# Values' products of all units in two parts, the feed-forward product in two parts beside them, shared banks by a fixed table

## The chip, the cores and the metric

The kernel runs on one core of a Trainium2 chip. Its five engines each run their own instruction stream, in order: TensorE (PE; its weight loads are PEld), VectorE (DVE), ScalarE (ACT), GpSimd (POOL) and SyncE (SP), which here issues DMAs. They wait for each other through semaphores. The metric is the device time of one execution in microseconds, median of several.

## The reference

One layer on x of shape (16, 512, 256), float32. After a layer norm without parameters, attention and a feed-forward product run side by side, and both are added to x:

```python
xn = _layernorm(x, axis=-1)
qkv = xn @ w_qkv.T + b_qkv                      # 16 heads of 16
att = einsum('bhqd,bhkd->bhqk', q, k) / sqrt(16) + hope_bias
att = softmax(where(causal, att, -inf))
attn = einsum('bhqk,bhkd->bhqd', att, v) @ w_proj.T + b_proj
ffn = fp8(bf16(xn) / s_in) @ fp8(kernel / s_k) * (s_in * s_k)   # rounded to bf16, + bias
out = x + attn + ffn
```

The position bias depends on the distance of query and key and on the head.

## The kernel before

The body of the loop handles one batch row b (of 16): the first is written out, a loop runs over bodies 1 to 13, and the last two are written out. A body has G = 4 units g (0 to 3) of four heads each, and a unit has SLOTS = 12 slots k. In each slot (g, k) TensorE computes two blocks: transposed scores of this unit (`scores_T`, L648, and L651 for the position features of units 0 and 1; banks scoreT_a, b, c in turn), which ScalarE turns into probabilities by an exponential (L1013), and plain scores for two units ahead (`scores`, L625; banks score_a, b, c in turn), of which VectorE takes the row maxima (L1101). Slots 0 to 3 have 512 columns, slots 4 to 7 384, slots 8 to 11 384 in two pieces. Slot k of either kind needs the exponential, or the maximum, of slot k - 3, which frees its bank. GpSimd masks the diagonal of the probabilities (L1324).

Between slots TensorE does jobs in two shared banks, misc_a and misc_b, whose slots stand in the tables `*_AT` at the head of the file:

- PV, the product of values and probabilities of the unit before (`pv`, L674; fp32, four heads beside each other in 32 columns each). Its first part (key tile 0, 512 columns) needs only the first mask; the rest (tiles 1 to 3) the other two. Each fp32 matmul leaves two records, so the first part has 8 and the rest 24. In unit 0 and unit 1 the first part stands behind slot 0 and the rest behind slot 3; in units 2 and 3 both stand behind slot 3.
- MT, the transposition of the next unit's row maxima (`job_MT`, L610 and L611). It waits for ScalarE's copy of them (`max_hi`, L908, ahead of the exponential of slot 2). In units 2 and 3 it is issued between the first part of PV and the rest, in unit 1 ahead of the rest, in unit 0 behind it. ScalarE copies it out (L914), SyncE sends it by DMA, and scores_T of the next unit wait for it.
- QK and V, projections of the next row (`job_QK`, `job_V`, L560), units 0, 1 and unit 2; FF, the feed-forward product (`job_FF`, L603), both halves behind slot 0 of unit 2; PJ, the output projection of the row before (`job_PJ`, L560), halves behind slots 0 and 6 of unit 3; T, transpositions of xn (`job_T`, L568), behind slot 9 of unit 3.

Each job waits until what the job before it left in its bank has been read (`misc`, `done`): for FF ScalarE's eviction (L1036), for PV ScalarE's `out_T` (L986, ahead of the exponential of slot 4), for PJ VectorE's addition to x (`result`, L1114, behind the maximum of slot 1 or 6), for V ScalarE's L887, for QK VectorE's L1089, for MT ScalarE's L914. The order of all jobs over a body is `ORDER`, and before, the two banks simply alternate along it. In units 2 and 3 that gives:

```
FF0 a, FF1 b | PV1 a, MT2 b | V0 a | V1 b || PJ0 a | PV2 b, MT3 a | PJ1 b | T0 a, T1 b
```

Of the kernel before, what the change touches and what calls it, by code (L numbers as in the profile page):

```python
# [27 lines left out]
B, T, C = 16, 512, 256  # L28
H, HD = 16, 16
TT = T // P  # L30
# [18 lines left out]

PV_AT = [(1, 0), (2, 3), (3, 3), (0, 0)]

PV_REST_AT = {0: (1, 3), 3: (0, 3)}
MT_AT, FIRST_MT_AT = [(0, 3), (1, 3), (2, 3), (3, 3)], (0, 2)
QK_AT = [(0, 6), (0, 9), (1, 6), (1, 9)]
V_AT = [(2, 6), (2, 9)]
FF_AT = [(2, 0), (2, 0)]
PJ_AT = [(3, 0), (3, 6)]
T_AT = (3, 9)  # L60

# [5 lines left out]
QK_HI_AT, QK_LO_AT = [(0, 6), (0, 9), (1, 6), (1, 9)], [(0, 7), (0, 10), (1, 7), (1, 10)]  # L67
V_OUT_AT = [(2, 6), (2, 9)]
AH_AT = [(2, 2), (2, 3)]
FF_OUT_AT = [(2, 0), (2, 1)]  # L70
RESULT_AT = [(3, 1), (3, 6)]
NORM_AT = [(3, 1), (3, 3), (3, 4), (3, 6)]
XH_AT = [(3, 9), (3, 10)]
# [7 lines left out]

FIRST_CHUNKS = [0, 1, 4, 5, 8, 9, 2, 3, 6, 7, 10, 11]

KINDS = ("PV", "MT", "QK", "V", "FF", "PJ", "T")
ORDER = [(KINDS[kind], i) for _, kind, i in sorted((at, kind, i) for kind, ats in enumerate(
    (PV_AT, MT_AT, QK_AT, V_AT, FF_AT, PJ_AT, [T_AT, T_AT])) for i, at in enumerate(ats))]
assert len(ORDER) % 2 == 0
MISC_BANK = {job: n % 2 for n, job in enumerate(ORDER)}
MASKED = -1.0e30
LEAST = -3.0e38  # L90

# [18 lines left out]
def due(jobs, g, k, lag=0):  # L110

    return [i for i, (jg, jk) in enumerate(jobs) if SLOTS * jg + jk == SLOTS * g + k - lag]
# [13 lines left out]
def build(nc, x, w_qkv, b_qkv, w_proj, b_proj, pos, ffn_w, s_in, s_k, ffn_b, feat_q, feat_k, out):  # L126
    with ExitStack() as ctx:
# [199 lines left out]
        def misc_of(kind, i):  # L327

            return MBS[MISC_BANK[kind, i]]

# [206 lines left out]
        def _(pe):  # L537
# [33 lines left out]
            def job_QK(b, m):  # L571

                col = P * [0, 2, 1, 3][m]
                if m == 0:
                    pe.wait_ge(xl_ready, 2 * (b + 1))
                bank = misc("QK", m, b - 1)
                split3(bank[:, :], (lambda ct: WH[:, ct, col:col + P], lambda ct: WL[:, ct, col:col + P]),
                       (lambda ct: XH[:, ct, :], lambda ct: XL[:, ct, :]), T).then_inc(qk_ready, 1)
# [84 lines left out]
            def pv(b, g, tiles, then):  # L663
                if 0 in tiles:
                    if g == 0:
                        pe.wait_ge(va_ready, b + 1)
                    misc("PV", g, b if g < 3 else b + 1)
                elif then and g < 3:
                    job_MT(*then)
                bank = misc_of("PV", g)  # L670
                for j in tiles:
                    pe.wait_ge(mask_done, 12 * b + 3 * g + min(j, 2) + 1)
                    for i in range(HU):
                        last = mm(bank[32 * i:32 * i + 32, P * j:T],  # L674
                                  VA[:, j, HU * g + i, :, :].rearrange("p d a -> p (d a)"),
                                  probs(g, j)[:, i, :], start=(j == 0), stop=(j == TT - 1))
                    if j == 0 and then:
                        job_MT(*then)
                if TT - 1 in tiles:
                    last.then_inc(pv_done, 1)  # L680
                if 0 not in tiles and then and g == 3:
                    job_MT(*then)
# [106 lines left out]
            def body(b, first, last, more):  # L789
                if not first and not last:  # L790
                    for n in range(2):
                        job = [x for x in ORDER if MISC_BANK[x] == n][-1]
                        bank_read[n] = done(*job, b - 1)
                for g in range(G):
                    nb, ng = (b, g + 2) if g < 2 else (b + 1, g - 2)
                    ahead = not (last and g >= 2)
                    for k in range(SLOTS):
                        pb, pg = (b, g - 1) if g else (b - 1, 3)
                        if ahead:
                            in_turn(scores_T(b, g, k, first), scores(nb, ng, k))  # L800
                        else:
                            in_turn(scores_T(b, g, k, first))
                        if not (first and g == 0):
                            then = None if last and g == 3 else (b, g + 1) if g < 3 else (b + 1, 0)
                            if (g, k) == PV_AT[pg]:
                                pv(pb, pg, range(1) if pg in PV_REST_AT else range(TT), None if pg in PV_REST_AT else then)
                            if pg in PV_REST_AT and (g, k) == PV_REST_AT[pg]:
                                pv(pb, pg, range(1, TT), then)
                        if first and (g, k) == FIRST_MT_AT:
                            job_MT(b, 1)  # L810
                        if last and (g, k) == LAST_DENOMINATORS_AT:
                            pe.wait_ge(max_done, ROW * B)
                            last_denominators(2)
                        if last and (g, k) == LAST_INVERSES_AT:
                            last_inverses(2)
                        if not last:
                            for i in due(QK_AT, g, k):
                                job_QK(b + 1, i)
                            for i in due(V_AT, g, k):
                                job_V(b + 1, i)  # L820
                        for i in due(FF_AT, g, k):
                            job_FF(b, i)
                        if not first:
                            for i in due(PJ_AT, g, k):
                                job_PJ(b - 1, i)
                        if (g, k) == T_AT and more:
                            for i in range(CT):
                                job_T(b + 2, i)
# [42 lines left out]
        def _(act):  # L871
# [122 lines left out]
            def body(b, first, last, more):  # L994
                for g in range(G):
                    for k in range(SLOTS):
                        pb, pg = (b, g - 1) if g else (b - 1, 3)
                        if (g, k) == FIRST_MAX_AT if first and g == 0 else k == MAX_AT:
                            if not (last and g == 3):
                                max_hi(*((b, g + 1) if g < 3 else (b + 1, 0)))  # L1000
                        if k == OUT_AT and not (first and g == 0):
                            if g == 0:
                                out_T(pb, pg, False)
                            if not (last and g == 3):
                                max_T(*((b, g + 1) if g < 3 else (b + 1, 0)))
                            if g > 0:
                                out_T(pb, pg, first and pg == 0)
                        act.wait_ge(st_ready, ROW * b + SLOTS * g + k + 1)
                        if first and (g, k) == (0, 4):
                            for i in range(2):  # L1010
                                act.wait_ge(feat_loaded[i], 64)
                        w = WJ[k // 4] if k < 8 else WJ[2] + WJ[3]
                        A(probs_slot(g, k), STB[(SLOTS * g + k) % 3][:, 0:w], ACT.Exp).then_inc(exp_done, 1)  # L1013
                        if first and (g, k) == FIRST_MT_OUT_AT:
                            max_T(b, 1)
                        if not last:
                            for i in due(QK_HI_AT, g, k):
                                QK_evac(b + 1, i)
                            for i in due(V_OUT_AT, g, k):
                                V_evac(b + 1, i)  # L1020
                        if more:
                            for t in due(NORM_AT, g, k):
                                normalise(b + 2, t)
                            for i in due(XH_AT, g, k):
                                XH_evac(b + 2, i)
                                if i == 0:
                                    act.wait_ge(xy_ready, b + 1)
                                XB_evac(b + 2, i)
                        if not first:
                            for ct in due(AH_AT, g, k):  # L1030
                                attn_hi(b - 1, ct)
                        for i in due(FF_OUT_AT, g, k):
                            act.wait_ge(ff_ready, 2 * b + i + 1)
                            if i == 0 and not last:
                                act.wait_ge(qz_done, b + 2)
                            A(Y1[:, 2 * i:2 * i + 2, :], misc_of("FF", i)[:, :].rearrange("p (t c) -> p t c", c=C),  # L1036
                              ACT.Identity, scale=SC[:, 3:4]).then_inc(y1_ready, 1)

            body(0, True, False, True)
            with act.Fori(1, B - 2) as b:  # L1040
# [449 lines left out]
```

## Time and profile before

| | us |
|---|---|
| median of 3 runs (766.87 to 767.3) | 767.23 |
| profiled execution | 769.2 |
| its span | 767.2 |
| TensorE busy | 738.7 |
| VectorE busy | 634.6 |
| ScalarE busy | 586.1 |
| GpSimd busy | 532.4 |

An engine is busy while an instruction of it runs; ends of matmuls are modelled, so start times say more of TensorE than its busy time. A row of the timeline is: start, duration in us, engine, line, operation, output <- inputs, shapes, count; in square brackets the engine's idle time ahead of it and what ended it.

### The profile page before, as it was taken

The page shows a single profiled execution, that of the slowest core. Times are in us where ns is not written, and L with a number is a line of the kernel's source. Part 1 is how long each engine was busy: PE and PEld are TensorE (multiplying, and loading weights), DVE is VectorE, ACT ScalarE, POOL GpSimd, SP SyncE. Part 2 cuts the span into 40 slices and gives each one's busy share as a digit, 9 for nine tenths or more (in the row PEclk, how much of TensorE's full clock was granted, in tenths as well). Part 3 has the DMA queues.
Part 4 walks back from the last instruction along what each step waited for, and adds up shares of the span by engine and source line. Part 5 has one row for each costly group of instructions (what it writes and reads, how often), then busy time and mean ns, then how long its engine had stood idle before and what let it go on. Part 6 is the DMA issues. An engine that isn't in the chain of part 4 may idle for free.

```text
span 767.2 us, 23128 instructions
## 1 busy us (share of the span) xinstructions
PE 738.7 (96%) x6285; PEld 475.1 (62%) x6285; DVE 634.6 (83%) x2401; ACT 586.1 (76%) x1263; POOL 532.4 (69%) x525
## 2 busy tenths in 40 slices
PE   7989999999999999999999999999999999999987
PEld 4656556666765666566566656666665666666555
DVE  4898798889989888988988898898988889888613
ACT  4557888787888878788887878878787888877662
POOL 7445767786777778776777868677776867767571
PEclk9999999999999999999999999999999999999889
DMA  5442353435335433533544253244425334443201
GB/s 181 150 152 103 128 176 142 139 118 178 117 138 174 153 127 118 184 128 121 174 153 141 112 187 136 108 170 152 158 95 193 133 120 153 160 148 108 88 32 62
DMA packets 55313, 105.65 MB, mean 138 GB/s; under 512 B 10421, under 2 KB 30389, under 8 KB 55285
## 3 DMA queue, kind: packets, MB, share of 16 engines
q1 hardware_dynamic: 53968, 104.52, 38.3%
q10 hardware_dynamic: 1316, 0.80, 0.4%
q8 instruction: 13, 0.21, 0.1%
q14 instruction: 16, 0.12, 0.1%
HBM read 18.42 MB, written 8.90 MB: 36 GB/s over the span
## 4 chain that ended last, share of the span: by engine, by line
PE 68%; ACT 11%; DVE 8%; issue 6%; DMA 2%; SPq 2%; DVEq 1%; ACTq 1%; POOLq 0%; POOL 0%
PE misc_a L560 13%; PE misc_a L674 10%; PE misc_b L560 9%; PE scoreT_b L648 9%; PE scoreT_a L648 5%; PE score_c L625 4%; PE misc_b L674 3%; ACT probs L1013 3%; PE score_a L625 2%; PE scoreT_b L651 2%; ACT qk_parts L901 2%; ACT attn_hi L992 2%; DVE row_max L1101 2%; SPq L351 1%; ACT out_T L986 1%
## 5 line engine op out<-in xcount | busy, mean ns | idle before, releaser
L1324 POOL TENSOR_SCALAR_AFFINE_SELECT probs<-probs 128x512 f32<-128x512 f32 x256 | 161.1, 640 | 185.7 <-ACT probs L1013 184.0
L1101 DVE CUSTOM_DVE_ANT_0 score_b<-score_b,causal_mask_q 128x384 f32<-128x384 f32 (+3 forms) x321 | 162.7, 523 | 80.6 <-PE score_b L625 80.3
L1101 DVE CUSTOM_DVE_ANT_0 score_a<-score_a,causal_mask_q 128x512 f32<-128x512 f32 x319 | 174.6, 563 | 2.9 <-PE score_a L625 2.8
L1101 DVE CUSTOM_DVE_ANT_0 score_c<-score_c,causal_mask_q 128x256 f32<-128x256 f32 (+3 forms) x384 | 172.0, 475 | 0.1
L1013 ACT ACTIVATE probs<-scoreT_b 128x384 f32<-128x384 f32 (+1 forms) x256 | 131.8, 515 | 44.7 <-PE scoreT_b L651 21.2
L1013 ACT ACTIVATE probs<-scoreT_a 128x512 f32<-128x512 f32 (+1 forms) x256 | 142.6, 557 | 9.3 <-PE scoreT_a L651 8.0
L1101 DVE DVE_READ_ACCUMULATOR2_ANT row_max<- 128x1 f32 x1024 | 142.8, 139 | 0.0
L1013 ACT ACTIVATE probs<-scoreT_c 128x384 f32<-128x384 f32 (+1 forms) x256 | 133.3, 521 | 1.5 <-PE scoreT_a L648 0.9
L674 PE MATMUL misc_a<-probs,v_ones 128*32 128x128 f32 (+3 forms) x1536 | 124.1, 441 | 3.5 <-DVE xnT_lo L1083 1.3
L648 PE MATMUL scoreT_b<-stacks 64*128 64x384 f32 (+3 forms) x320 | 120.6, 396 | 1.6 <-ACT probs L1013 1.5
L625 PE MATMUL score_b<-stacks 64*128 64x384 f32 (+3 forms) x321 | 116.0, 394 | 0.0
L648 PE MATMUL scoreT_a<-stacks 64*128 64x512 f32 (+3 forms) x320 | 106.6, 353 | 5.5 <-issue 2.1
L625 PE MATMUL score_a<-stacks 64*128 64x512 f32 x319 | 107.9, 370 | 0.3
L648 PEld LDWEIGHTS scoreT_b<-stacks 64*128 64x128 f32 x320 | 56.6, 184 | 77.4 <-ACT probs L1013 45.1
L648 PE MATMUL scoreT_c<-stacks 64*128 64x256 f32 (+3 forms) x384 | 102.4, 299 | 0.3 <-ACT probs L1013 0.3
L625 PE MATMUL score_c<-stacks 64*128 64x256 f32 (+3 forms) x384 | 94.5, 299 | 0.9 <-DVE row_max L1101 0.8
L674 PEld LDWEIGHTS misc_a<-probs,v_ones 128*32 128x32 f32 x1536 | 40.2, 109 | 54.0 <-issue 32.8
L648 PEld LDWEIGHTS scoreT_c<-stacks 64*128 64x128 f32 x384 | 68.6, 186 | 1.2 <-ACT probs L1013 0.9
L625 PEld LDWEIGHTS score_c<-stacks 64*128 64x128 f32 x384 | 65.5, 186 | 5.7 <-DVE row_max L1101 4.4
L625 PEld LDWEIGHTS score_a<-stacks 64*128 64x128 f32 x319 | 54.5, 186 | 15.6 <-DVE row_max L1101 11.1
L648 PEld LDWEIGHTS scoreT_a<-stacks 64*128 64x128 f32 x320 | 57.2, 186 | 11.2 <-issue 5.0
L625 PEld LDWEIGHTS score_b<-stacks 64*128 64x128 f32 x321 | 54.2, 184 | 1.4 <-DVE row_max L1101 1.1
(238 smaller groups left out, 1937.4 us busy)
## 6 DMA issues: line engine op xcount, KB each, us to landing
stacks<-qk_parts SPq DMA_DIRECT2D x128, 512.0 KB, 3.7
x_ring<-in_L_attn_x SPq DMA_DIRECT2D x16, 512.0 KB, 3.6
attn<-out_T SPq DMA_DIRECT2D x63, 128.0 KB, 2.6
xn<-recips SPq DMA_DIRECT2D x31, 256.0 KB
out<-x_ring SPq DMA_DIRECT2D x15, 512.0 KB, 3.0
stacks<-neg_max_T SPq DMA_DIRECT2D x128, 4.0 KB
low_features<-neg_max_T SPq DMA_DIRECT2D x126, 4.0 KB
low_features<-probs SPq DMA_DIRECT2D x8, 128.0 KB, 4.3
```

Source lines behind the costliest of these rows:

```text
L351: eng.dma_start(max_rows(g, h), MTS[2 * TT * h:2 * TT * h + 2 * TT, g % 2, :].bitcast(F32)) \
L560: last = mm(o, l(ct), r(ct), start=(ct == 0 and i == 0), stop=(ct == CT - 1 and i == 2))
L625: last = mm(SB_[n % 3][:, o:o + w], STK[rows, u, 0, P * qt:P * qt + P], STK[rows, u, 1, 0:w], start=True, stop=True)
L648: last = mm(bank, STK[rows, u, 1, P * j:P * j + P], STK[rows, u, 0, P * j:T], start=True, stop=(g >= 2))
L651: last = mm(bank, EXT[rows, u, 1, P * j:P * j + P], EXT[rows, u, 0, P * j:T], start=False, stop=True)
L674: last = mm(bank[32 * i:32 * i + 32, P * j:T], VA[:, j, HU * g + i, :, :].rearrange("p d a -> p (d a)"), probs(g, j)[:, i, :], start=(j == ...
L901: A(qk_part(m, 0), misc_of("QK", m)[:, :].unsqueeze(1).broadcast_to([P, 2, T]), ACT.Identity, bias=BQ[:, bias:bias + 1]).then_inc(qh_ready, 1)
L986: A(OT[:, :], misc_of("PV", g)[:, :], ACT.Copy).then_inc(ot_ready, 1)
L992: A(AH[:, ct, :], attn_row(b)[:, ct, :], ACT.Copy).then_inc(ah_ready, 1)
L1013: A(probs_slot(g, k), STB[(SLOTS * g + k) % 3][:, 0:w], ACT.Exp).then_inc(exp_done, 1)
L1101: last = V.tensor_tensor_reduce(bank, bank, CMQ[:, T - w:T], 1.0, LEAST, ALU.add, ALU.max, MX[:, g % 2, 8 * h + 4 + qt:8 * h + 5 + qt])
L1324: last = GP.affine_select(out=d, in_=d, compare_op=ALU.is_ge, fill=0.0, base=0, pattern=[[0, HU], [1, P]], channel_multiplier=-1)
```

## The change

All four products of values are in two parts: the first part behind slot 0, the rest behind slot 3. MT is issued with the rest (ahead of it in units 1 to 3, behind it in unit 0). The second half of the feed-forward product and its eviction move from slots (2, 0) and (2, 1) to (2, 6); it stands ahead of the values' projection there, and its eviction ahead of ScalarE's other evictions. The banks come from a table in place of the alternation; PV is always in misc_a, MT, FF and PJ in misc_b. Units 2 and 3 become:

```
PV1 a, FF0 b | MT2 b | FF1 b, V0 a | V1 b || PV2 a, PJ0 b | MT3 b | PJ1 b | T0 a, T1 b
```

```diff
-PV_AT = [(1, 0), (2, 3), (3, 3), (0, 0)]
-PV_REST_AT = {0: (1, 3), 3: (0, 3)}
+PV_AT = [(1, 0), (2, 0), (3, 0), (0, 0)]
+PV_REST_AT = [(1, 3), (2, 3), (3, 3), (0, 3)]
-FF_AT = [(2, 0), (2, 0)]
+FF_AT = [(2, 0), (2, 6)]
-FF_OUT_AT = [(2, 0), (2, 1)]
+FF_OUT_AT = [(2, 0), (2, 6)]
-KINDS = ("PV", "MT", "QK", "V", "FF", "PJ", "T")
+KINDS = ("PV", "MT", "QK", "FF", "V", "PJ", "T")
-MISC_BANK = {job: n % 2 for n, job in enumerate(ORDER)}
+MISC_BANK = {(kind, i): bank for kind, banks in (("PV", (0, 0, 0, 0)), ("MT", (1, 1, 1, 1)), ("QK", (0, 1, 0, 1)), ("FF", (1, 1)),
+                                                 ("V", (0, 1)), ("PJ", (1, 1)), ("T", (0, 1))) for i, bank in enumerate(banks)}
...
                             if (g, k) == PV_AT[pg]:
-                                pv(pb, pg, range(1) if pg in PV_REST_AT else range(TT), None if pg in PV_REST_AT else then)
-                            if pg in PV_REST_AT and (g, k) == PV_REST_AT[pg]:
+                                pv(pb, pg, range(1), None)
+                            if (g, k) == PV_REST_AT[pg]:
                                 pv(pb, pg, range(1, TT), then)
...
+                        for i in due(FF_AT, g, k):
+                            job_FF(b, i)
+                        if not last:
                             for i in due(V_AT, g, k):
                                 job_V(b + 1, i)
-                        for i in due(FF_AT, g, k):
-                            job_FF(b, i)
...
                         A(probs_slot(g, k), STB[(SLOTS * g + k) % 3][:, 0:w], ACT.Exp).then_inc(exp_done, 1)
...
+                        for i in due(FF_OUT_AT, g, k):
+                            act.wait_ge(ff_ready, 2 * b + i + 1)
+                            ...
                         if not last:
                             for i in due(QK_HI_AT, g, k):
                                 QK_evac(b + 1, i)
...
                                 attn_hi(b - 1, ct)
-                        for i in due(FF_OUT_AT, g, k):
-                            ...
```

## Rows read from the trace of the kernel before

**Rows 1.** The profile's page: busy time, granted clock in 40 slices, chain by engine.
```profile
PE 738.7 (96%) x6285; PEld 475.1 (62%) x6285; DVE 634.6 (83%) x2401; ACT 586.1 (76%) x1263; POOL 532.4 (69%) x525
...
PEclk9999999999999999999999999999999999999889
...
PE 68%; ACT 11%; DVE 8%; issue 6%; DMA 2%; SPq 2%; DVEq 1%; ACTq 1%; POOLq 0%; POOL 0%
```
**Rows 2.** Waits of TensorE: us in total, times, longest.
```profile
PE misc_a L610 <- DVE x_ring L1114: 2.3, 14, 0.2
```
**Rows 3.** Timeline of TensorE: the transpositions T that close two neighbouring bodies.
```profile
262.23 0.66 PE L568 MATMUL misc_a<-ident_f,xn 128*128 128x128 f32 x4
...
306.67 0.66 PE L568 MATMUL misc_a<-ident_f,xn 128*128 128x128 f32 x4
```
**Rows 4.** Timeline of TensorE, a body's unit 3, slots 0 to 3.
```profile
298.07 0.38 PE L560 MATMUL misc_a<-w_projT_hi,attn_hi 128*128 128x256 f32 x1
298.29 0.28 PE L560 MATMUL misc_a<-w_projT_lo,attn_hi 128*128 128x256 f32 x1
...
299.68 0.50 PE L625 MATMUL score_b<-stacks 64*128 64x512 f32 x1
...
300.58 1.06 PE L674 MATMUL misc_b<-probs,v_ones 128*32 128x512 f32 x8
301.81 0.27 PE L610 MATMUL misc_a<-ident_f,row_max 128*32 128x128 f32 x1 [0.16 <-DVE x_ring L1114]
...
302.06 1.50 PE L674 MATMUL misc_b<-probs,v_ones 128*32 128x384 f32 x24
```
**Rows 5.** Timeline of VectorE and ScalarE in the same unit.
```profile
300.36 0.70 DVE L1101 CUSTOM_DVE_ANT_0 score_b<-score_b,causal_mask_q 128x512 f32<-128x512 f32 x1 [0.55 <-PE score_b L625]
300.97 0.69 DVE L1114 TENSOR_TENSOR x_ring<-misc_a,x_ring 128x512 f32 x1
301.20 0.22 ACT L908 ACTIVATE row_max_hi<-row_max 128x32 fp32r<-128x32 f32 x1
...
304.11 0.57 DVE L1101 CUSTOM_DVE_ANT_0 score_b<-score_b,causal_mask_q 128x384 f32<-128x384 f32 x1 [1.14 <-PE score_b L625]
```
**Rows 6.** Timeline of TensorE, unit 1: first part of PV behind slot 0.
```profile
276.01 1.07 PE L674 MATMUL misc_a<-probs,v_ones 128*32 128x512 f32 x8
277.00 0.50 PE L648 MATMUL scoreT_b<-stacks 64*128 64x512 f32 x1
```
**Rows 7.** Timeline of unit 2, slots 0 to 6: TensorE, ScalarE and VectorE.
```profile
287.06 0.61 PE L603 MATMUL misc_a<-ffn_w_q,xq 128*128 128x256 bf16 x4
...
287.86 0.61 PE L603 MATMUL misc_b<-ffn_w_q,xq 128*128 128x256 bf16 x4 [0.20 <-DVE qk_parts L1089]
...
288.40 0.49 PE L648 MATMUL scoreT_b<-stacks 64*128 64x512 f32 x1
...
288.93 0.60 ACT L1013 ACTIVATE probs<-scoreT_b 128x512 f32<-128x512 f32 x1 [0.16 <-PE scoreT_b L648]
...
289.08 0.70 DVE L1101 CUSTOM_DVE_ANT_0 score_b<-score_b,causal_mask_q 128x512 f32<-128x512 f32 x1
...
289.43 0.68 ACT L1036 ACTIVATE xnT_bf<-misc_b,ffn_scales 128x512 bf16<-128x512 f32 x1
...
290.00 0.23 ACT L908 ACTIVATE row_max_hi<-row_max 128x32 fp32r<-128x32 f32 x1
...
290.57 0.28 PE L610 MATMUL misc_b<-ident_f,row_max 128*32 128x128 f32 x1
...
292.73 0.34 PE L648 MATMUL scoreT_a<-stacks 64*128 64x384 f32 x1
...
293.20 0.39 PE L560 MATMUL misc_a<-w_qkvT_hi,xnT_hi 128*128 128x256 f32 x1
```
**Rows 8.** Timeline of the first body's unit 3.
```profile
78.07 0.26 ACT L908 ACTIVATE row_max_hi<-row_max 128x32 fp32r<-128x32 f32 x1
...
79.39 0.28 PE L610 MATMUL misc_a<-ident_f,row_max 128*32 128x128 f32 x1
```
**Rows 9.** Timeline of TensorE, the last body's unit 3, slot 0.
```profile
738.55 0.79 PE L648 MATMUL scoreT_a<-stacks 64*128 64x512 f32 x1 [0.93 <-DMA stacks<-neg_max_T]
```

More of the change, by code:

```diff
@@ L82 @@
 FIRST_CHUNKS = [0, 1, 4, 5, 8, 9, 2, 3, 6, 7, 10, 11]
-KINDS = ("PV", "MT", "QK", "V", "FF", "PJ", "T")
+KINDS = ("PV", "MT", "QK", "FF", "V", "PJ", "T")
 ORDER = [(KINDS[kind], i) for _, kind, i in sorted((at, kind, i) for kind, ats in enumerate(
-    (PV_AT, MT_AT, QK_AT, V_AT, FF_AT, PJ_AT, [T_AT, T_AT])) for i, at in enumerate(ats))]
-assert len(ORDER) % 2 == 0
-MISC_BANK = {job: n % 2 for n, job in enumerate(ORDER)}
+    (PV_AT, MT_AT, QK_AT, FF_AT, V_AT, PJ_AT, [T_AT, T_AT])) for i, at in enumerate(ats))]
+MISC_BANK = {(kind, i): bank for kind, banks in (("PV", (0, 0, 0, 0)), ("MT", (1, 1, 1, 1)), ("QK", (0, 1, 0, 1)), ("FF", (1, 1)),
+                                                 ("V", (0, 1)), ("PJ", (1, 1)), ("T", (0, 1))) for i, bank in enumerate(banks)}
 MASKED = -1.0e30
@@ L1015, in body @@
                             max_T(b, 1)
+                        for i in due(FF_OUT_AT, g, k):
+                            act.wait_ge(ff_ready, 2 * b + i + 1)
+                            if i == 0 and not last:
+                                act.wait_ge(qz_done, b + 2)
+                            A(Y1[:, 2 * i:2 * i + 2, :], misc_of("FF", i)[:, :].rearrange("p (t c) -> p t c", c=C),
+                              ACT.Identity, scale=SC[:, 3:4]).then_inc(y1_ready, 1)
                         if not last:
@@ L1031, in body @@
                                 attn_hi(b - 1, ct)
-                        for i in due(FF_OUT_AT, g, k):
[L1033 to L1037, printed above, removed]
             body(0, True, False, True)
```

## Prediction

> **What bounds the kernel now.** The profile's page first. TensorE is busy for 96% of the span and holds 68% of the chain that ended last, at full clock everywhere but near the end [rows 1]. The list of TensorE's own waits has one entry that matters here: fourteen times the transposition of the row maxima (L610, in misc_a) waits 0.2 us for VectorE's addition at L1114 [rows 2]. The timeline gives the body of the loop: from the transpositions that close one body to those of the next is 306.67 - 262.23 = 44.44 us [rows 3]. A body has four units of twelve slots. In most of them TensorE starts a job right behind the last, and ScalarE and VectorE follow it; so whatever TensorE issues more, or waits for longer, lengthens the body, unless it stood idle there anyway. I therefore follow TensorE's start times through units 2 and 3, where all edits lie.
>
> **Unit 3 (the third unit's product of values).** Before, slot 0 is followed by the first half of the projection (298.07); slot 1's scores start at 299.68; slots 1 to 3 take 0.90; at 300.58 comes the first part of the product (8 records), at 301.81 the transposed maxima (MT), at 302.06 the rest [rows 4]. What releases MT is a chain that starts at slot 1's scores: VectorE takes their maximum at 300.36, then adds the projection to x at 300.97 (0.69), and 0.15 behind its end MT starts, since MT takes the bank that the projection used. VectorE had been idle 0.55 before that maximum, waiting for the scores [rows 5]. ScalarE's leg is nearly as long: the copy of the maxima starts at 301.20, takes 0.22, and with the same 0.15 allows MT at 301.57 [rows 5]. So from slot 1's scores to MT are 301.81 - 299.68 = 2.13 us, and the first part of the product was hidden in them. TensorE waited only 0.16.
>
> The change puts that first part behind slot 0, ahead of the projection, and MT ahead of the rest. Both are in misc_b's chain again (projection's half, then MT), so the wait for L1114 stays. What the first part costs at slot 0 is seen in unit 1, where it stands there already: 277.00 - 276.01 = 0.99 [rows 6]. Slot 1 therefore starts 1.0 later. The 2.13 us from there to MT belong to VectorE and ScalarE and do not shrink; only their cover is gone: TensorE has 0.90 of scores and then waits about 1.23. MT, and all behind it, comes 1.0 later. Nothing behind it gives that back: VectorE is idle for 1.14 before slot 4's maximum, waiting for TensorE [rows 5]. Sum of unit 3: +1.0. Bounds: if VectorE's leg ran faster ScalarE's would bind, 0.24 earlier, so +0.75; if the 1.23 from the first part's start to MT [rows 4] were all lost, +1.23. I take 1.0, since unit 1 has the same instructions in the same place.
>
> **Unit 2 (the second unit's product, feed-forward product).** Before: both halves of the feed-forward product behind slot 0, 287.06 and 287.86, the second after a wait of 0.20 for VectorE; slot 1 at 288.40; MT at 290.57 behind the first part; slot 6's scores at 292.73; values' projection at 293.20 [rows 7]. A half costs 288.40 - 287.86 = 0.54. After: first part 287.06 to 288.05, one half to 288.6 (its bank, misc_b, is free by then, so the wait of 0.20 goes), slot 1 at 288.6, 0.2 later than before. ScalarE evicts the half from about 288.75, and by the starts of rows 7 (an eviction 290.00 - 289.43 = 0.57, an exponential 289.43 - 288.93 = 0.50) copies the maxima at 288.75 + 0.57 + 0.50 = 289.82, which allows MT 0.37 later (0.22 and 0.15), at 290.19. That is 0.38 earlier than before, though TensorE has idled some 0.65 for it. Not all of it is kept: slot 6's scores need slot 3's maximum, VectorE's maxima run back to back there (289.08 right behind the one before), and slot 1's is now 0.2 late. I estimate slot 6 at 292.5, so 0.2 are left of the 0.38. Behind it stands the second half of the feed-forward product, 0.54 less the change of shape (0.1, below) that the values' projection next to it no longer pays, and less the 0.13 that TensorE stood there before the values' projection (293.20 - 292.73 = 0.47 for a block of 0.34): +0.3. I take +0.1 for the unit. Bounds: -0.38 if the second half is wholly hidden, +0.54 if nothing hides it.
>
> **The rest.** Units 0 and 1 have had the product in two parts already, and their jobs keep their banks. In unit 3 the second half of the projection moves behind MT in misc_b, where it waited for the product's eviction before: nothing to a few hundredths. ScalarE's second eviction of the feed-forward product moves to slot 6, into the time it waits for the values; the wait for a free bank that it adds there is for a value written long before. GpSimd's bias addition (L1330) stands behind a mask of slot 7, after slot 6's eviction. SyncE's queue keeps its order; the maxima it sends come 0.4 earlier in unit 2 and 1.0 later in unit 3, with the unit that wants them as far behind as before.
>
> **Ends.** The projection exists from the second body on, and the last body has no MT in unit 3: fourteen bodies pay unit 3, the number of rows 2. In the first body MT (79.39) comes 1.3 after the copy of the maxima at 78.07 [rows 8], so that unit had slack and the first part moves free of charge: +0.1 for unit 2 alone. In the last body unit 3 starts behind a wait for the sent maxima (0.93, [rows 9]), which ScalarE's later copy passes on: +0.3, with half-clock stretches near the end that can fall differently, 3 us either way.
>
> Sum: 14 x (1.0 + 0.1) + 0.1 + 0.3 = 15.8 us. The profiled execution took 769.2 (span 767.2), the timed ones 767.23; the sum is small beside both, so 769.2 becomes 785.0 and the median 783.0.
>
> **A rule against the change.** The first matmul of the projection is followed after 0.22 (298.07 to 298.29), while all twelve take 1.61 [rows 4], 0.126 for each of the others: a change of tile shape costs about 0.1. The Trainium skill, TensorEngine Tiling, Key Properties, says that changing the tiling mode drains TensorE; the trace agrees. By that rule each of units 2 and 3 pays one more change, 14 x 2 x 0.1 = 2.8 us. In my sum unit 3's is inside the 0.99 and unit 2's inside a wait; paid on top in unit 2 it would make 784.4.
>
> **Rivals.** (a) The first part moves into a hole. In the first body it does [rows 8]. Were TensorE also idle around slot 0 in the full bodies, unit 3 would lose nothing and unit 2 keep its 0.38: 14 x -0.38 = -5.3, 761.9. It decides if the longer wait for MT in unit 3 is under 0.4. Against it: VectorE idle 0.55 before slot 1's maximum waits on TensorE, not the reverse [rows 5]. 4%. (b) The loss is given back in slots 4 to 11, no change: VectorE and ScalarE would have to be the late ones there, and the 1.14 says the opposite. 3%. (c) The fixed table makes new waits: feed-forward, values, projection and MT now follow each other in misc_b, each behind an eviction, and nothing of unit 2 is hidden: 14 x (1.0 + 0.54) + 0.4 = 22, 789.2. Between each pair lie at least three slots or a first part. 10%. (d) The clock. A wait of 0.93 in the last body is followed by a block of scores of 0.79 where the same block takes 0.49 [rows 7, 9], that is at half clock; a slice of 19.2 us with the digit 8 [rows 1] holds 4 to 8 us of it. A wait of 1.23 in each body might do the same: up to 3 us of doubled work each, 14 x 3 + 16 = 58, 825. For it speaks only that row; around unit 3 TensorE is otherwise full. 5%. (e) Unit 3's chain shortens and unit 2 gains: 14 x (0.75 - 0.38) = 5, 772.6. 5%.
>
> **Numbers.** My forecast, 779 to 787: 73%. Range 775 to 790: it takes in most of (c), and leaves out (a), (b), (d) and (e), about 17 in 100. What this kernel's measurement can tell from no change is 0.2%, 1.5 us. Faster 4% (a), same 3% (b), slower 93%.
>
> **What would show it.** In unit 3 the first part directly behind slot 0; the gap between slot 3's scores and MT about 1.2 us, released by L1114; 2.1 us from slot 1's scores to MT. In unit 2 MT about 3.1 us behind slot 0's job, released by ScalarE's copy, where it was 3.51. A body of 45.5 us. I am wrong if MT in unit 3 starts under 1.8 us behind slot 1's scores, if the body is under 44.9, or if the granted clock leaves 1.0 in the loop.

## The result, and the profile after

| | before | after |
|---|---|---|
| median, us | 767.26 (766.87 to 768.08, 4 runs) | 792.01 (787.52 to 797.75, 4 runs) |
| profiled execution, us | 769.2 | 793.55 |
| its span, us | 767.2 | 791.8 |
| body of the loop, us | 44.44 | 45.4 in most, 47.1 in others |

The ratio is 1.0325, interval [1.0255, 1.0396]: 24.8 us slower. I had said 783.0 and a range of 775 to 790, so the direction was right, and the size was not. And the changed kernel spreads over 10 us in four runs, where the one before spread over 1.2 (and over 6.7 in the 25 runs beside e5 to e8).

The page after, against [rows 1]: busy times, granted clock, chain.

```profile
PE 742.1 (94%) x6285; PEld 480.4 (61%) x6285; DVE 644.5 (81%) x2401; ACT 585.2 (74%) x1263; POOL 527.6 (67%) x525
...
PEclk9999999999999999999999999999999999999889
...
PE 80%; issue 6%; ACT 5%; DVE 5%; DMA 2%; SPq 2%; DVEq 0%; POOL 0%; ACTq 0%; POOLq 0%
```

The number of instructions is the same. The page shows little more: TensorE's share fell by two points, VectorE is busy 10 us longer although it does nothing new. That is the first hint at something other than waits. TensorE's waits after (engine, tile, line, what it waited for; us in total, times, longest), against [rows 2]:

```profile
PE misc_b L611 <- DVE x_ring L1116: 16.3, 14, 1.2
PE misc_b L611 <- ACT row_max_hi L910: 9.9, 19, 0.7
PE score_b L626 <- DVE row_max L1103: 3.4, 6, 0.6
```

(Lines from L611 on are one or two further down than before.) The first row is [rows 2] grown from 2.3 to 16.3 us, 1.2 for each of the same fourteen bodies: the wait that the prediction put there. The second was 0.5 before: it is mostly MT of unit 2, which now waits for ScalarE's copy (0.54 in the body shown below); the sum had allowed 0.65 for that. The third is new and was in no rival of mine: six times slot 7's scores of unit 2 wait for a maximum. The bodies, from the transpositions that close one to the next:

```profile
219.38 0.55 PE L569 MATMUL misc_a<-ident_f,xn 128*128 128x128 f32 x3
...
266.48 0.33 PE L569 MATMUL misc_a<-ident_f,xn 128*128 128x128 f32 x1
...
311.86 0.66 PE L569 MATMUL misc_a<-ident_f,xn 128*128 128x128 f32 x4
```

The second body takes 45.38 us, 0.94 more than before; the first 47.10, another 1.72. Four bodies of the profiled execution take 47.0 to 47.2 and a fifth 48.56; a sixth of the kind stands behind the last of these transpositions, so there are six in fourteen.

**Unit 3 after**, TensorE, VectorE and ScalarE, against [rows 4, 5]:

```profile
302.32 1.06 PE L675 MATMUL misc_a<-probs,v_ones 128*32 128x512 f32 x8
303.32 0.38 PE L561 MATMUL misc_b<-w_projT_hi,attn_hi 128*128 128x256 f32 x1
...
304.93 0.49 PE L626 MATMUL score_b<-stacks 64*128 64x512 f32 x1
...
305.60 0.70 DVE L1103 CUSTOM_DVE_ANT_0 score_b<-score_b,causal_mask_q 128x512 f32<-128x512 f32 x1 [1.53 <-PE score_b L626]
306.21 0.69 DVE L1116 TENSOR_TENSOR x_ring<-misc_b,x_ring 128x512 f32 x1
306.44 0.22 ACT L910 ACTIVATE row_max_hi<-row_max 128x32 fp32r<-128x32 f32 x1
307.05 0.27 PE L611 MATMUL misc_b<-ident_f,row_max 128*32 128x128 f32 x1 [1.17 <-DVE x_ring L1116]
...
309.36 0.57 DVE L1103 CUSTOM_DVE_ANT_0 score_b<-score_b,causal_mask_q 128x384 f32<-128x384 f32 x1 [1.14 <-PE score_b L626]
```

The first part costs 1.00 ahead of the projection; from slot 1's scores to MT are 2.12 (before 2.13), with nothing in them but scores; VectorE's idle time at slot 1 grew from 0.55 to 1.53, and at slot 4 it is 1.14 as before, so nothing came back.

**Unit 2 after**, a body of the short kind, against [rows 7]; the last two rows are VectorE's second quantisation step and GpSimd's subtraction:

```profile
291.30 1.07 PE L675 MATMUL misc_a<-probs,v_ones 128*32 128x512 f32 x8
292.30 0.61 PE L604 MATMUL misc_b<-ffn_w_q,xq 128*128 128x256 bf16 x4
292.84 0.50 PE L649 MATMUL scoreT_b<-stacks 64*128 64x512 f32 x1
...
293.03 0.69 ACT L1022 ACTIVATE xnT_bf<-misc_b,ffn_scales 128x512 bf16<-128x512 f32 x1 [0.58 <-PE misc_b L604]
...
294.09 0.23 ACT L910 ACTIVATE row_max_hi<-row_max 128x32 fp32r<-128x32 f32 x1
...
294.45 0.28 PE L611 MATMUL misc_b<-ident_f,row_max 128*32 128x128 f32 x1 [0.54 <-ACT row_max_hi L910]
...
297.12 0.61 PE L604 MATMUL misc_b<-ffn_w_q,xq 128*128 128x256 bf16 x4
...
296.56 0.69 DVE L1132 SCALAR_TENSOR_TENSOR quant_work<-xn,quant_work 128x512 f32<-128x512 f32 x1
...
296.56 2.93 POOL L1365 TENSOR_TENSOR attn_lo<-attn,attn_hi 128x1024 fp32r<-128x1024 f32 x1
```

MT is 3.15 behind slot 0's job, before 3.51: 0.36 earlier, where I had 0.38. Slot 6's scores come 5.46 behind it (before 5.67, forecast 5.44) and the values' projection 6.19 (before 6.14). The whole body is 0.94 longer, the sum's 1.1 less 0.16.

**The collision.** The same two instructions in a body of the kernel before, with GpSimd's mask ahead of them, and in one of the long kind after, with the maximum and the scores that follow:

```profile
291.85 0.64 POOL L1324 TENSOR_SCALAR_AFFINE_SELECT probs<-probs 128x512 f32<-128x512 f32 x1 [0.92 <-ACT probs L1013]
...
292.12 0.92 DVE L1130 SCALAR_TENSOR_TENSOR quant_work<-xn,quant_work 128x512 f32<-128x512 f32 x1
...
292.47 2.82 POOL L1363 TENSOR_TENSOR attn_lo<-attn,attn_hi 128x1024 fp32r<-128x1024 f32 x1
```

```profile
249.54 2.38 POOL L1365 TENSOR_TENSOR attn_lo<-attn,attn_hi 128x1024 fp32r<-128x1024 f32 x1
...
249.57 2.90 DVE L1132 SCALAR_TENSOR_TENSOR quant_work<-xn,quant_work 128x512 f32<-128x512 f32 x1
252.39 0.55 DVE L1103 CUSTOM_DVE_ANT_0 score_b<-score_b,causal_mask_q 128x384 f32<-128x384 f32 x1
...
253.06 0.44 PE L626 MATMUL score_b<-stacks 64*128 64x384 f32 x1 [0.53 <-DVE row_max L1103]
```

Both instructions read two operands from SBUF, the memory on the chip that the program keeps its tiles in. The one that starts later is held up by the other. Before, VectorE's step starts 0.35 ahead of the subtraction, and the subtraction is drawn out from 2.38 to 2.82, which nobody waits for; it ends 2.25 behind the step's end. That the step takes 0.92 there and not 0.69 is a smaller collision of the same kind, with the mask: the mask is running when the step starts, and the step ends 0.55 behind the mask's end (291.85 + 0.64 = 292.49, against 293.04). In e10 one step takes 0.94 with the mask alone beside it, since the subtraction is held back there. After, the subtraction starts 0.03 ahead and takes 2.38, and VectorE's step takes 2.90, 2.2 more than its 0.69, and ends 0.55 behind the subtraction's end. The maxima of slots 4 to 6 stand behind it, and TensorE's slots 7 and 8 behind those.

The edits brought the two together. Counted from the job behind slot 0 of unit 2, VectorE's step started at 292.12 - 287.06 = 5.06 and GpSimd's at 5.41 before; after (the short body above) both at 296.56 - 291.30 = 5.26. VectorE comes 0.20 later, since slot 1's scores do, and GpSimd 0.15 earlier, since ScalarE is no longer held by the second eviction of the feed-forward product: a margin of 0.35 became 0.00. The subtraction follows the mask directly, so what decides is whether the step starts before the mask is over: 0.37 before its end in the kernel before, at its very end now. Which one wins then changes from body to body and run to run: six bodies of fourteen here. The spread between runs follows it: four runs spread over 5.0 us in e1, which still has the collision, and over some 2 in e5 and e9, which have not.

### The profile page after: what moved, and what is told of

It reads as the page before. It is cut to its first block, busy times and chain, and to the rows that moved or that the text cites. A ratio compares the mean times of both kernels' runs of the same rounds, so it can differ in the third digit from the quotient of the medians.

```text
span 791.8 us, 23128 instructions
## 1 busy us (share of the span) xinstructions
PE 742.1 (94%) x6285; PEld 480.4 (61%) x6285; DVE 644.5 (81%) x2401; ACT 585.2 (74%) x1263; POOL 527.6 (67%) x525
## 4 chain that ended last, share of the span: by engine, by line
PE 80%; issue 6%; ACT 5%; DVE 5%; DMA 2%; SPq 2%; DVEq 0%; POOL 0%; ACTq 0%; POOLq 0%
PE misc_a L675 19%; PE misc_b L561 15%; PE scoreT_b L649 10%; PE misc_a L561 8%; PE scoreT_a L649 6%; PE score_c L626 4%; PE score_a L626 3%; PE scoreT_b L652 2%; PE misc_b L611 2%; PE misc_b L604 2%; PE scoreT_a L652 1%; PE scoreT_c L652 1%; ACT probs L1015 1%; DVE xnT_lo L1085 1%; PE scoreT_c L649 1%
## 5 line engine op out<-in xcount | busy, mean ns | idle before, releaser
L675 PE MATMUL misc_a<-probs,v_ones 128*32 128x512 f32 (+3 forms) x2048 | 166.3, 442 | 3.5 <-POOL probs L1326 1.1
L1103 DVE DVE_READ_ACCUMULATOR2_ANT row_max<- 128x1 f32 x1024 | 145.5, 142 | 0.0
L626 PE MATMUL score_a<-stacks 64*128 64x512 f32 x319 | 109.7, 375 | 0.4
L649 PE MATMUL scoreT_c<-stacks 64*128 64x256 f32 (+3 forms) x384 | 104.0, 302 | 0.3 <-ACT probs L1015 0.3
L675 PEld LDWEIGHTS misc_a<-probs,v_ones 128*32 128x32 f32 x2048 | 53.6, 109 | 70.2 <-issue 45.2
L988 ACT ACTIVATE out_T<-misc_a 128x512 f32<-128x512 f32 x64 | 38.0, 593 | 34.2 <-PE misc_a L675 34.2
```

The lines of the kernel that those rows point to most:

```text
L626: last = mm(SB_[n % 3][:, o:o + w], STK[rows, u, 0, P * qt:P * qt + P], STK[rows, u, 1, 0:w], start=True, stop=True)
L649: last = mm(bank, STK[rows, u, 1, P * j:P * j + P], STK[rows, u, 0, P * j:T], start=True, stop=(g >= 2))
L675: last = mm(bank[32 * i:32 * i + 32, P * j:T], VA[:, j, HU * g + i, :, :].rearrange("p d a -> p (d a)"), probs(g, j)[:, i, :], start=(j == ...
L988: A(OT[:, :], misc_of("PV", g)[:, :], ACT.Copy).then_inc(ot_ready, 1)
L1103: last = V.tensor_tensor_reduce(bank, bank, CMQ[:, T - w:T], 1.0, LEAST, ALU.add, ALU.max, MX[:, g % 2, 8 * h + 4 + qt:8 * h + 5 + qt])
```

## The experiments

All are compared with the kernel before on the same chip; its medians there were 767.1 (e1 to e4), 768.2 (e5 to e8) and 768.7 (e9, e10). Ratios have their 95% interval behind them.

**e1: unit 3 put back.**
```
-PV_AT = [(1, 0), (2, 0), (3, 0), (0, 0)]
-PV_REST_AT = [(1, 3), (2, 3), (3, 3), (0, 3)]
+PV_AT = [(1, 0), (2, 0), (3, 3), (0, 0)]
+PV_REST_AT = {0: (1, 3), 1: (2, 3), 3: (0, 3)}   # and the two calls of pv as before
```


> The changed kernel with unit 3 put back alone: the product of unit 2's probabilities is whole behind slot 3 again, MT between its first part and the rest. Theory: unit 3's lost cover costs 1.0 us in each of 14 bodies, so 13 to 14 us less than the changed kernel (792.0), about 778 with a clean body of about 44.5 us. What is above 767.3 + 1.4 (unit 2's 0.1 in 14 bodies) = 768.7 is the second cost: the collision of VectorE's second quantisation step (L1132) with GpSimd's subtraction (L1365), which stays, since unit 2 is untouched: 1.6 us in each body where GpSimd starts first. Rival (the added cost comes from the clock after unit 3's longer wait): then it goes with the wait, and the time is 768 to 770 with hardly any spread.

777.87 us (775.59 to 780.57), 1.0136 [1.0085, 1.0187]. In the trace the wait of MT for L1116 is back at 2.3 us, the short bodies take 44.4, and the long kind is still there (four steps of 2.9). So the two losses are separate, and the second belongs to unit 2. Four steps at some 1.7 are 7 of the 10.7 us; one of the long bodies takes 47.65 and has a stretch at half clock behind its step (a granted clock of 0.87 over 290 to 300 us), and the rest lies at the ends of the program.

**e2: VectorE's steps one slot earlier.**
```
-MAGIC_AT, FIRST_MAGIC_AT = [(2, 1), (2, 2), (2, 3)], ...
+MAGIC_AT, FIRST_MAGIC_AT = [(2, 0), (2, 1), (2, 2)], ...
```


> The changed kernel with VectorE's three quantisation steps one slot earlier (behind the maxima of slots 0, 1, 2 of unit 2 in place of 1, 2, 3), so that the last is over before GpSimd's subtraction starts. Theory (the two engines exclude each other on operands in SBUF, and the later one waits for the whole of the other's instruction): no such step longer than 1.0 us, all bodies at 45.4 us, 782 to 783.5 us and runs within 1 us of each other. Rival (clock or DMA makes the slow bodies): 788 to 798 as before, bodies of 47 us remain.

789.99 us (787.33 to 790.29), 1.0285 [1.0240, 1.0331]. In eleven bodies the step takes 0.69 and the subtraction 2.38, and the two no longer meet. In the other three the step starts during the mask and takes 1.11 to 1.15, and these are the three longest bodies (46.6 to 46.7). So the collision with the subtraction no longer delays VectorE; but the time is not what I expected (782 to 783.5). I had overlooked that now all three steps stand ahead of slot 3's maximum, which slot 6's scores need:

```profile
PE score_a L626 <- DVE row_max L1103: 5.5, 10, 0.9
```

The bodies take 45.7 to 46.7. This wait is 5.5 of the 9.8 us by which the run lies above e5; the rest was not followed up. By its time this run lies where the rival had put it; by the steps' lengths it speaks for the collision.

**e3: the collision made in the kernel before.**
```
-MAGIC_AT, FIRST_MAGIC_AT = [(2, 1), (2, 2), (2, 3)], ...
+MAGIC_AT, FIRST_MAGIC_AT = [(2, 1), (2, 2), (2, 4)], ...
```


> The kernel before with VectorE's last quantisation step behind the maximum of slot 4 in place of slot 3, so that GpSimd's subtraction starts ahead of it in every body. Theory: in every body from the second on the step takes 2 to 3 us in place of 0.9 and TensorE waits about 0.6 to 1.2 us in slots 7 and 8: 776 to 784 us. Rival (the stretch has nothing to do with GpSimd): the step keeps its 0.7 to 0.9 us and the time stays at 767 to 768.

787.70 us (786.10 to 788.48), 1.0270 [1.0227, 1.0313]; every body is 45.8. The pair in one of them (all fourteen are alike, 2.00 to 2.06):

```profile
251.04 2.39 POOL L1363 TENSOR_TENSOR attn_lo<-attn,attn_hi 128x1024 fp32r<-128x1024 f32 x1
```
```profile
251.92 2.06 DVE L1130 SCALAR_TENSOR_TENSOR quant_work<-xn,quant_work 128x512 f32<-128x512 f32 x1
```

It starts 0.88 behind GpSimd's and ends 0.55 behind its end, as in the changed kernel. None of the change is in this kernel, so the mechanism stands by itself. It costs 1.35 us a body here, some 20 us in all, more than the 776 to 784 that I expected.

**e4: the addition ahead of slot 1's maximum, kernel before.**
```
-RESULT_AT = [(3, 1), (3, 6)]
+RESULT_AT = [(3, 0), (3, 6)]
```


> The kernel before with VectorE's addition of the projection's first half (L1114) ahead of the maximum of slot 1 in place of behind it. Theory: MT in unit 3 is released by VectorE's leg; without it ScalarE's leg and the end of the product's first part, both at about 301.57 in place of 301.81, let it go: 0.2 us in each of 14 bodies, 764 to 765 us, and the wait of L610 for L1114 is gone. Rival (ScalarE's leg is the one that binds, or slot 1's later maximum costs elsewhere): 766.5 to 768.

765.18 us (763.07 to 767.47), 0.9967 [0.9948, 0.9986]; bodies of 44.25, and MT follows the first part's end:

```profile
298.78 1.06 PE L674 MATMUL misc_b<-probs,v_ones 128*32 128x512 f32 x8
299.78 0.28 PE L610 MATMUL misc_a<-ident_f,row_max 128*32 128x128 f32 x1
```

1.00 in place of 1.23 [rows 4]: VectorE's leg was the one that bound.

**e5: GpSimd held behind VectorE, changed kernel.**
```
                     if g == 2 and not first:
+                        if not last:
+                            wait_alone(pool, (ident_steps, 3), (qm_done, 2 * (b + 2)))
                         attn_parts(b - 1)
```


> The changed kernel; GpSimd's subtraction of the attention parts (L1365) in unit 2 waits in addition until VectorE's two quantisation steps are done, so it can never start ahead of the second. Nothing else moves. Theory: no step longer than 1.0 us, every body at 45.4 us, 782 to 783.5 us on a chip where the kernel before takes 767.2, spread about that of the kernel before. Rival (the clock or TensorE's own queue makes the 47 us bodies): 788 to 793, bodies of 47 us remain.

780.18 us (779.22 to 781.30), 1.0148 [1.0120, 1.0175], some 12 below the changed kernel, with a spread of 2 us in place of 10. All bodies are 45.4 to 45.7. The time is below the 782 to 783.5 that I expected. GpSimd waits 0.7 and nobody misses it:

```profile
250.35 2.40 POOL L1365 TENSOR_TENSOR attn_lo<-attn,attn_hi 128x1024 fp32r<-128x1024 f32 x1 [0.71 <-DVE quant_work L1132]
```
```profile
249.52 0.68 DVE L1132 SCALAR_TENSOR_TENSOR quant_work<-xn,quant_work 128x512 f32<-128x512 f32 x1
```

**e6: e5 with unit 3 put back** (the edits of e1 and e5).

> The same, with unit 3 put back as well (its product whole behind slot 3): what is left of the change is unit 2's split product and split feed-forward product, without the collision. Theory: the sum's term for unit 2, 0.1 us in 14 bodies, or nothing: 767.5 to 769, bodies of 44.4 to 44.6. Rival (unit 2's edits cost by themselves, by their additional changes of shape): 771 to 775.

767.68 us (765.93 to 770.65), 0.9996 [0.9975, 1.0017]: unit 2's edits cost nothing and bring nothing.

**e7: both legs to MT short, kernel before** (e4's edit, and ScalarE's first normalisation one slot later).
```
-NORM_AT = [(3, 1), (3, 3), (3, 4), (3, 6)]
+NORM_AT = [(3, 2), (3, 3), (3, 4), (3, 6)]
```


> The kernel before with the addition of the projection's first half ahead of slot 1's maximum (as in the earlier run) and the first normalisation of unit 3 behind the exponential of slot 2 in place of slot 1, so that ScalarE's leg to MT is 0.5 shorter too. Theory: with both legs short TensorE's own first part of the product binds; MT leaves with its end, another 0 to 0.05 us per body: 764 to 765. Rival (ScalarE's leg still held MT): another 0.1 to 0.2 per body, 762 to 763.

765.76 us (762.88 to 768.88), 0.9965 [0.9944, 0.9985]; bodies of 44.24: no more than e4.

**e8: both legs short, changed kernel** (the edits of e4, e5 and e7).

> The changed kernel with GpSimd held behind VectorE, and with both legs to MT in unit 3 shortened as in the run on the kernel before. Theory: in the changed kernel nothing covers the legs, so all that they lose is gained: from slot 1's scores to MT 1.4 to 1.5 us in place of 2.12, 0.65 us in each of 14 bodies, 773 to 774.5 us. Rival (the loss in unit 3 is TensorE's own work for the first part and its changes of shape, not the bare chain): 781 to 783.

770.17 us (767.36 to 772.62), 1.0026 [1.0007, 1.0044]. From slot 1's scores to MT it is 1.30 in place of 2.12, 0.82 less, where I expected 1.4 to 1.5 (and 773 to 774.5 us). MT now waits for ScalarE's copy:

```profile
299.99 0.50 PE L649 MATMUL scoreT_b<-stacks 64*128 64x512 f32 x1
...
301.29 0.28 PE L611 MATMUL misc_b<-ident_f,row_max 128*32 128x128 f32 x1 [0.34 <-ACT row_max_hi L910]
```

The same edits are worth 0.2 us a body in the kernel before and 0.75 here: with the first part gone from slot 3, the chain is bare, and nearly all that it loses is gained.

**e9: unit 2 put back, unit 3 as changed.**
```
-PV_AT = [(1, 0), (2, 0), (3, 0), (0, 0)]
+PV_AT = [(1, 0), (2, 3), (3, 0), (0, 0)]
-PV_REST_AT = [(1, 3), (2, 3), (3, 3), (0, 3)]
+PV_REST_AT = {0: (1, 3), 2: (3, 3), 3: (0, 3)}   # and the two calls of pv as before
-FF_AT, FF_OUT_AT = [(2, 0), (2, 6)], [(2, 0), (2, 6)]
+FF_AT, FF_OUT_AT = [(2, 0), (2, 0)], [(2, 0), (2, 1)]   # banks a, b
```


> The changed kernel with unit 2 put back alone: its product whole behind slot 3 and both halves of the feed-forward product behind slot 0, evicted from misc_a and misc_b as before. GpSimd is not held back. Theory: unit 3 costs 0.9 to 1.0 us in 14 bodies and nothing collides, since unit 2's times, and with them the order of VectorE's step and GpSimd's subtraction, are those of the kernel before: 780 to 782, no step over 1.1 us, all bodies at 45.4. Rival (unit 3's longer wait brings the collisions about): bodies of 47 us and 788 or more.

780.55 us (779.58 to 781.55), 1.0161 [1.0137, 1.0185]; bodies of 45.4, no step over 0.95 (those of about 0.9 start during the mask, as in the kernel before). All thirty of VectorE's steps together, in the changed kernel and here (count | busy us, mean ns | idle before):

```profile
L1132 DVE SCALAR_TENSOR_TENSOR quant_work<-xn,quant_work 128x512 f32<-128x512 f32 x30 | 34.0, 1132 | 0.0
```
```profile
L1132 DVE SCALAR_TENSOR_TENSOR quant_work<-xn,quant_work 128x512 f32<-128x512 f32 x30 | 24.0, 799 | 0.0
```

Unit 3's longer wait does not bring the collisions with the subtraction about.

**e10: unit 2 changed, GpSimd held, unit 3 as before, both legs short** (e6 with the edits of e4 and e7).

> The best that the experiments point to: unit 2 of the change with GpSimd held behind VectorE, unit 3 as before, and both legs to MT in unit 3 shortened. Theory: unit 2 is worth nothing (767.7 against 768.2) and the legs 0.2 us in 14 bodies: 764 to 766, a body of 44.2. Rival (unit 2's split gains once unit 3 no longer waits): under 763.

764.29 us (763.34 to 766.00), 0.9948 [0.9928, 0.9969]: the fastest here, faster than both kernels. Whether unit 2's part of it gains anything over e7 is open, since the intervals overlap.

The four corners, as ratios to the kernel before:

| | unit 3 as before | unit 3 changed |
|---|---|---|
| unit 2 as before | 1 | 1.0161 (e9) |
| unit 2 changed, GpSimd held | 0.9996 (e6) | 1.0148 (e5) |
| unit 2 changed | 1.0136 (e1) | 1.0325 |

## Why the prediction was wrong, step by step

- **Unit 3, +1.0 in fourteen bodies: right.** MT waits 1.17 for L1116, fourteen times; the chain kept its length (2.12); the short body is 45.38. By time the term is 12 us (e5, e9), 0.86 for each of the bodies.
- **Unit 2, +0.1: right as an account of TensorE.** MT came 0.36 earlier, slot 1 0.2 later, as written; together nothing (e6, 767.68 against 768.21, where 1.4 was forecast). The rule on drains could have cost another 1.4; no run shows such a cost (e6's interval reaches 1.3 us).
- **The failed step** is the term of +0.1 for unit 2, with what the paragraph on the rest put at nothing: "slot 1's is now 0.2 late" and ScalarE earlier by the eviction that leaves were both in it, and both were priced on TensorE's path alone. I never put VectorE's and GpSimd's own instructions beside each other. The two shifts (0.20 later, 0.15 earlier) used up the 0.35 by which VectorE's second step had started ahead of GpSimd's subtraction, and the later of that pair is held up by the other. It costs 1.6 to 1.8 us a body where GpSimd wins. The unit's edits cost some 13 us beside the changed unit 3 (1.0325 against e9's 1.0161) and 10.7 without it (e1), where 1.4 was forecast. Over the profiled execution this makes 13.2 (fourteen times 0.94) + 6 x 1.72 = 23.5 of 24.35 us. The remainder is larger than it looks, since its parts have different signs: the first bodies take 1.3 less than before, the body with a stretch at half clock (below) 1.5 more, and the end of the program 0.9 more.
- **Rival (d), the clock,** was not the cause. It has a small share: in the last of the long bodies of the loop the wait is followed by matmuls at half clock, a mean of 0.83 over ten microseconds:

```profile
665.00:675.00 10.00, 9.40 (x61) 6.76 (x60) 8.06 (x28) 6.21 (x13) 6.00 (x5) 0.83 0.08 28
```

(From, to, length; busy time of PE, PEld, DVE, ACT, POOL; granted clock, DMA share, GB/s.) In the other five long bodies the clock stays at 1.00. The wait of rival (d) is not what did it: in e5 and e9 MT waits for L1116 fourteen times as here, and the loop keeps its clock throughout. Nor does every collision do it: e3 has fourteen of them and keeps its clock too. What makes the difference is open. Rivals (a), (b) and (e) did not happen, nor did (c), whose 789.2 is near the measured time by accident: among TensorE's waits no job in misc_b but MT waits for its bank. (The time given for (e) is 0.2 off: 14 x 0.37 makes 772.4.)

What the trace of the kernel before had to offer: VectorE's second step takes 0.92 there and the first 0.69, the same instruction on the same shape, and GpSimd's subtraction 2.82 in the loop but 2.35 in the last body, where VectorE has no such step. The excess is the overlap: the step's with the mask ahead of it (in all fourteen bodies it ends 0.54 to 0.55 behind the mask), the subtraction's with the step. The Trainium skill, SBUF — State Buffer, section Who interferes with whom, has the rule: a VectorE instruction with two SBUF inputs contends with a GpSimd instruction that reads SBUF, and issue order decides who blocks. The traces agree, with 2.90 and 2.06 against 0.69 where GpSimd was first, and 2.82 to 2.93 against 2.38 where VectorE was.

## What to carry to other kernels

- A wait is worth what it covers: before moving work from in front of a waiting instruction, measure the chain that releases it from its first event, and check what else lies in it. Work taken from the cover costs its full length, however early it is done.
- When an edit shifts two engines against each other, list the pairs of VectorE and GpSimd instructions on SBUF that stood within the shift of each other. If their order is not held by a semaphore, a small shift can turn it; here 0.35 us were enough. A wait that fixes the order cost nothing here (e5) and took out 12 us and nearly all of the spread.
- Instructions of one form with different durations, and a spread that grew, are the marks of such a pair.

## What the runs showed that I had not expected

The later of the two instructions does not share; it ends at a fixed time behind the end of the earlier. VectorE's step ends 0.55 behind the subtraction, whether it started 0.03 (2.90 us) or 0.88 (2.06 us) after it. It also ends 0.54 to 0.55 behind GpSimd's mask, an instruction with one operand, when it starts well before the mask's end: 0.92 us in the kernel before, 1.15 in three bodies of e2. The other way round, GpSimd's subtraction ends 2.25 behind VectorE's step (2.82 and 2.93 us against 2.38). In both orders this is the later one's own time (0.69, 2.38) less about 0.14.

The order turns within hundredths of a microsecond. In the profiled execution of the changed kernel the subtraction starts 0.01 to 0.06 ahead in the six bodies where it wins, and at the same time or 0.09 behind in the eight where VectorE does, so that identical bodies of one execution fall on either side.
